# The causal mask in a decoder layer's self scores: sixteen bf16 products on 32 rows in place of four on 128

## The chip, the cores and the metric

The kernel runs on one core of a Trainium2 chip. The metric is the time of one execution on the device in microseconds (us). The profiled execution gives a span, from its first to its last instruction; the time of a run is longer by what lies around the span.

## The reference

One decoder layer over 32 batch rows of 128 tokens and 512 features: self attention with 16 heads of 32 features, rotary positions and a causal mask; cross attention to a context with fake int8 quantisation; a mixture of 64 experts with the best 8 for each token. Each of the three adds its result to its input. The part that matters:

```python
q = _rope(proj(Wq, bq)); k = _rope(proj(Wk, bk)); v = proj(Wv, bv)
att = jnp.einsum('bhqd,bhkd->bhqk', q, k) / scale
causal = jnp.tril(jnp.ones((t, t), bool))
att = jnp.where(causal, att, -jnp.inf)
att = jax.nn.softmax(att, axis=-1)
```

## The kernel before

The kernel has three stages. A setup loads the weights, splits most of them into a high and a low part, and loads small constants. The attention stage does one batch row (128 tokens on 128 partitions) a turn, 32 in all, with the work of several rows interleaved: a turn `cur` does the projections of row cur-1, the self attention of cur-2, the cross attention of cur-3 and cur-4, and the routing of cur-4 and cur-5. The expert stage then walks the 64 experts. It reads rows that GpSimd has scattered to `routed` in HBM, and adds the results to the output by indirect DMAs.

Each engine runs an order written out by hand in its `body(cur)`: on TensorE `turn_keys`, `positions`, `weigh_cross_1`, `turn_queries`, `turn_x`, `weigh_cross_3`, `_0`, `_2`, `turn_cross_keys`, `self_scores`, `turn_cross_attention`, `cross_values_b`, `turn_quantised_x` and so on. An engine waits on a semaphore where a step needs another engine's work (`reached`). The turns 1 to 6 and the last five are written out, those between are a loop.

The helper `scores` (L511) makes the scores of four groups of four heads in four banks of PSUM, 512 columns each: head 4i+j lies in bank j, columns 128i to 128i+127. Features of group j lie on partitions 32j to 32j+31, so the score products (L520) work on strips of 32 rows, one for each j, with fp32 operands, and stand in the profile with two records each. For the self scores (banks 2, 6, 3, 7) the mask comes first: L515 multiplies the identity `idb`, moving and read four times over, with the weights `mask_add` (128x128, bf16, 0 or -1e30), and starts the accumulation of each bank; the sixteen score products add to it. The cross scores (`wide_b`) have no mask.

Other lines that the prediction speaks of: L484 transposes in fp32, L489 transposes in bf16, L502 the fp32 projections, L508 the bf16 ones, L527 transposes of the probabilities, L534 their products with the values, and L545 and L546 the counts of positions. On VectorE L1269 takes the maximum of a bank of scores, L1311 and L1314 make the sum x2 behind the cross attention's output (`cross_scores` of TensorE waits for it), and L1479 and L1483 quantise x for `turn_quantised_x`. On ScalarE L1036 copies the turned cross keys. On GpSimd L1798 casts three constants to bf16 in the setup; TensorE waits for all of them (`s_init`) before its second turn. L1725 is a cast of the context. SP issues the loads: the constants behind the first four weight matrices, and later the filling of `routed` (`empty_row`, four DMAs of 5120 KB).

Of the kernel before, what the change touches and what calls it, by code (L numbers as in the profile page):

```python
# [31 lines left out]
BF16 = mybir.dt.bfloat16  # L32
# [5 lines left out]
P = 128  # L38
B = 32
D = 512  # L40
KT = D // P
H = 16
DH = D // H
# [59 lines left out]
def layer(nc, x, ctxT_in, qT_w, kT_w, vT_w, oT_w, xkT_w, xvT_w, xq_w, xp_w, biases, vb, xkb, xvb, ob, xbq, xbp, routerT,  # L103
# [4 lines left out]
    def sb(name, shape, dt=F32):  # L108
        return st.enter_context(nc.sbuf_tensor(name, shape, dt))
# [4 lines left out]
    with st:  # L114
# [6 lines left out]

        idf = sb("idf", [P, P])
        idb = sb("idb", [P, P], BF16)
        mask_add = sb("mask_add", [P, P], BF16)
        before = sb("before", [P, P], BF16)
        ones_b = sb("ones_b", [P, P], BF16)
        ones_f = sb("ones_f", [P, P])
        cos_sb = sb("cos_sb", [P, DH])
        sin_sb = sb("sin_sb", [P, DH])
        slot_base = sb("slot_base", [P, E])  # L130
# [42 lines left out]
        with ExitStack() as attention_only:  # L173
            def early(name, shape, dt=F32):
                return attention_only.enter_context(nc.sbuf_tensor(name, shape, dt))

            for name in ("q", "k", "v", "xk", "o", "xv"):
                W[name] = tuple(early(f"w_{name}_{part}", [P, KT, D], F32R) for part in ("hi", "lo"))
            roped = early("roped", [P, 2 * D])
            qT = early("qT", [P, NG, P])  # L180
            v_sb = early("v_sb", [P, D])
            xk_sb = early("xk_sb", [P, D])
            ctx_sb = early("ctx_sb", [P, D])
            turned_bias = early("turned_bias", [P, 2 * D])
            xv_bias = early("xv_bias", [P, D])
            xq_wT = early("xq_wT", [P, KT, D], BF16)
            xq8 = early("xq8", [P, D], BF16)
            xq8T = early("xq8T", [P, KT, P], BF16)
            att_bias = early("att_bias", [P, D])
            xv_sb = early("xv_sb", [P, D])  # L190
            probsT = early("probsT", [P, NG, GH * P])
            xp_wT = early("xp_wT", [P, KT, D], BF16)
            xo_tmp = early("xo_tmp", [P, D])[:, :]
            xo8 = early("xo8", [P, D], BF16)
            xo8T = early("xo8T", [P, KT, P], BF16)
            wide_a = early("wide_a", [P, 4 * D])
            row = early("row", [P, ROW])
# [149 lines left out]
        def _(sp):  # L347
# [12 lines left out]
            def load_constants():  # L360
                for dst, src_c in ((cos_sb, cos_t), (sin_sb, sin_t), (slot_base, slot0)):
                    sp.dma_start(dst[:, :], src_c).then_inc(s_const, 16)
                for k, src_c in enumerate((causal, prior)):
                    sp.dma_start(x3T[:, k * P:(k + 1) * P], src_c).then_inc(s_const, 16)
                sp.dma_start(xq_bs[:, :], xbq.rearrange("(g p) -> p g", p=P),
                             allow_slow_non_contiguous=True).then_inc(s_const, 16)
                sp.dma_start(v_bias[:, :], vb.rearrange("(g p) -> p g", p=P),
                             allow_slow_non_contiguous=True).then_inc(s_const, 16)
                sp.dma_start(xk_bias[:, :], xkb.rearrange("(g p) -> p g", p=P),
                             allow_slow_non_contiguous=True).then_inc(s_const, 16)  # L370
                sp.dma_start(xv_bias[:, :], xvb.unsqueeze(0).to_broadcast([P, D])).then_inc(s_const, 16)
                sp.dma_start(xatt[:, :], ob.unsqueeze(0).to_broadcast([P, D])).then_inc(s_const, 16)
                sp.dma_start(xp_bias[:, :], xbp.unsqueeze(0).to_broadcast([P, D])).then_inc(s_const, 16)
                sp.dma_start(router_w[:, :, :], routerT.rearrange("(t p) e -> p t e", p=P)).then_inc(s_const, 16)
# [105 lines left out]
        def _(pe):  # L480
# [30 lines left out]
            def scores(banks, q, keys, masked, done):  # L511

                if masked:
                    for b in banks:
                        pe.matmul(bank[:, b, :], idb[:, :], mask_add[:, :].unsqueeze(1).to_broadcast([P, GH, P]),  # L515
                                  start=True, stop=False)
                for i in range(NG):
                    for j, b in enumerate(banks):
                        own = slice(j * DH, (j + 1) * DH)
# [333 lines left out]
            def turn_quantised_weights():  # L853
# [17 lines left out]
                pe.wait_ge(s_wprep, 3)  # L871
                pe.wait_ge(s_att, 1)
                for g in range(KT):
                    last = pe.matmul(bank[:, 7, g * P:(g + 1) * P], ones_f[:, :], xn2[:, g * P:(g + 1) * P],
                                     start=True, stop=True)
                last.then_inc(s_wT, 1)

# [837 lines left out]
        def _(pool):  # L1715
# [72 lines left out]
            pool.iota(empty_row[:, D:ROW:2], pattern=[[0, E]], base=TOKENS, channel_multiplier=1,  # L1788
                      allow_small_or_imprecise_dtypes=True).then_inc(s_init2, 1)
            pool.memset(ones_b[:, :], 1.0).then_inc(s_init, 1)  # L1790
            pool.memset(ones_f[:, :], 1.0).then_inc(s_init, 1)
            pool.memset(chosen_before[:, :], 0.0).then_inc(s_init, 1)

            body(1)
            pool.wait_ge(s_ident, 16)
            pool.wait_ge(s_const, 16 * N_CONST)
            for dst, src in ((idb[:, :], idf[:, :]), (mask_add[:, :], x3T[:, 0:P]), (before[:, :], x3T[:, P:2 * P])):
                pool.tensor_copy(dst, src).then_inc(s_init, 1)  # L1798

            body(2)  # L1800
# [36 lines left out]
def tables():  # L1837
# [6 lines left out]
        "cos_t": np.concatenate([cos, cos], 1).astype(np.float32),  # L1844
        "sin_t": np.concatenate([-sin, sin], 1).astype(np.float32),
        "ident_f": np.eye(P, dtype=np.float32),
        "causal": np.where(p[None, :] > p[:, None], MASKED, 0.0).astype(np.float32),
        "prior": (p[:, None] < p[None, :]).astype(np.float32),
        "slot0": np.tile(np.float32(NOWHERE) - CAP * np.arange(E, dtype=np.float32), (P, 1)).astype(np.float32),
    }  # L1850
# [29 lines left out]
```

## Time and profile before

| | |
|---|---|
| time, median of 3 runs | 1783.19 us (1775.75 to 1784.44) |
| span of the profiled execution | 1569.0 us |
| TensorE (PE) busy | 1406.8 us, 90% |
| its weight loads (PEld) | 1063.2 us, 68% |
| VectorE (DVE) busy | 1168.0 us, 74% |
| ScalarE (ACT) busy | 971.5 us, 62% |
| GpSimd (POOL) busy | 673.1 us, 43% |
| mean granted clock of TensorE | 0.960 of full speed |
| mask products L515 | 128 records, 33.7 us busy |
| chain that ended last | PE 65%, DMA 23%, issue 5%, DVE 4% |

The shares are means over the three stages: setup and filling to about 100 us, attention to about 1100 us, experts to the end. Matmuls are pipelined: a record's duration includes the way through the array, so what one costs is read from the distance between starts, or from the chain, not from its duration.

### The profile page before, as it was taken

The page shows a single profiled execution, that of the slowest core. Times are in us where ns is not written, and L with a number is a line of the kernel's source. Part 1 is how long each engine was busy: PE and PEld are TensorE (multiplying, and loading weights), DVE is VectorE, ACT ScalarE, POOL GpSimd, SP SyncE. Part 2 cuts the span into 40 slices and gives each one's busy share as a digit, 9 for nine tenths or more (in the row PEclk, how much of TensorE's full clock was granted, in tenths as well). Part 3 has the DMA queues.
Part 4 walks back from the last instruction along what each step waited for, and adds up shares of the span by engine and source line. Part 5 has one row for each costly group of instructions (what it writes and reads, how often), then busy time and mean ns, then how long its engine had stood idle before and what let it go on. Part 6 is the DMA issues. An engine that isn't in the chain of part 4 may idle for free.

```text
span 1569.0 us, 35603 instructions
## 1 busy us (share of the span) xinstructions
PE 1406.8 (90%) x10963; PEld 1063.2 (68%) x10996; DVE 1168.0 (74%) x3111; ACT 971.5 (62%) x3345; POOL 673.1 (43%) x654
## 2 busy tenths in 40 slices
PE   3699999999999999999999999998619887888895
PEld 2467777777777777777777777776516565655573
DVE  5678889998999989999899999889524444444453
ACT  3357777777777777777777777777504333333342
POOL 0012444444444344453444534544343544555566
PEclk9799999999999999999999999999759999999997
DMA  9861332322111100111010111000597999999964
GB/s 283 347 237 35 131 125 101 105 98 107 66 46 45 34 27 27 34 34 40 27 27 27 34 43 30 27 21 21 191 331 214 292 249 287 281 276 281 261 99 51
DMA packets 159738, 195.81 MB, mean 125 GB/s; under 512 B 39541, under 2 KB 121845, under 8 KB 159680
## 3 DMA queue, kind: packets, MB, share of 16 engines
q1 hardware_dynamic: 120768, 157.27, 30.9%
q0 software_dynamic: 38912, 37.87, 11.8%
q8 instruction: 24, 0.39, 0.1%
q14 instruction: 34, 0.28, 0.1%
HBM read 127.60 MB, written 130.29 MB: 164 GB/s over the span
## 4 chain that ended last, share of the span: by engine, by line
PE 65%; DMA 23%; issue 5%; DVE 4%; ACT 1%; POOL 1%; SPq 1%; POOLq 0%; DVEq 0%
PE bank L502 33%; DMA out<-x,slots 20%; PE bank L527 7%; PE bank L484 7%; PE bank L520 5%; PE bank L534 4%; PE bank L508 3%; PE bank L540 2%; PE bank L515 2%; DMA x_in<-in_x 1%; PE bank L489 1%; DMA wide_b<-in_xkT_w 1%; POOL routed L1753 1%; DMA probsT<-in_oT_w 1%; ACT probs L966 1%
## 5 line engine op out<-in xcount | busy, mean ns | idle before, releaser
L966 ACT ACTIVATE probs<-bank,small 128x128 f32<-128x128 f32 x1024 | 362.1, 377 | 51.0 <-DVE small L1269 47.8
L1753 POOL DMA_INDIRECT routed<-row,slots x248 | 252.7, 1019 | 133.8 <-issue 74.0
L1822 POOL DMA_INDIRECT out<-x,slots x128 | 199.3, 1557 | 197.6 <-DMA out<-x,slots 137.4
L1718 POOL TENSOR_TENSOR small<-small,half 128x1 f32<-128x1 f32 x96 | 54.4, 567 | 523.3 <-DVE small L1241 523.3
L966 ACT ACTIVATION_READ_ACCUMULATOR probs<-bank,small 128x1 f32 x1024 | 220.7, 216 | 0.0
L960 ACT ACTIVATE probsT<-bank 128x512 f32<-128x512 f32 x256 | 144.1, 611 | 89.1 <-PE bank L527 89.1
L1269 DVE TENSOR_REDUCE small<-bank 128x4 f32<-128x512 f32 x256 | 166.7, 682 | 35.4 <-PE bank L520 35.4
L527 PE MATMUL bank<-idf,probs 128*128 128x128 f32 x1024 | 147.2, 277 | 2.4 <-ACT probs L966 2.4
L1673 DVE TENSOR_SCALAR slots<-pairs 128x1 uint32<-128x1 f32 x128 | 13.7, 149 | 174.7 <-DMA out<-x,slots 171.1
L527 PEld LDWEIGHTS bank<-idf,probs 128*128 128x128 f32 x1024 | 122.2, 144 | 26.8 <-DVE probs L1278 3.5
L1199 ACT ACTIVATE xn<-bank 128x192 f32<-128x192 f32 x64 | 21.3, 332 | 146.4 <-PE bank L906 146.4
L906 PE MATMUL bank<-w_gate_up,x_in 128*128 128x384 f32 x256 | 94.2, 514 | 0.3 <-issue 0.3
L1278 DVE TENSOR_TENSOR probs<-probs,small 128x512 f32<-128x512 f32 x128 | 89.9, 702 | 4.4
L906 PE MATMUL bank<-w_gate_up,x_res 128*128 128x384 f32 x256 | 92.6, 507 | 0.0
L906 PEld LDWEIGHTS bank<-w_gate_up,x_in 128*128 128x128 f32 x256 | 49.0, 202 | 29.7 <-issue 6.4
L906 PEld LDWEIGHTS bank<-w_gate_up,x_res 128*128 128x128 f32 x256 | 48.6, 200 | 27.9 <-issue 4.5
L502 PE MATMUL bank<-w_q_hi,xT_hi 128*128 128x512 f32 x128 | 57.7, 451 | 0.7 <-ACT xT_hi L960 0.7
L502 PE MATMUL bank<-w_o_hi,attT_hi 128*128 128x512 f32 x132 | 52.7, 399 | 3.5 <-DVE attT_lo L1626 2.4
L1679 DVE TENSOR_SCALAR x<-bank,pairs 128x256 f32<-128x256 f32 x128 | 55.4, 475 | 0.0
L502 PE MATMUL bank<-w_xv_hi,cT_hi 128*128 128x512 f32 x128 | 53.9, 421 | 0.4 <-ACT wide_b L1036 0.4
L502 PE MATMUL bank<-w_v_hi,xT_hi 128*128 128x512 f32 x128 | 54.0, 422 | 0.0
L502 PE MATMUL bank<-w_xk_hi,cT_hi 128*128 128x512 f32 x128 | 53.4, 417 | 0.0
(242 smaller groups left out, 3843.4 us busy)
## 6 DMA issues: line engine op xcount, KB each, us to landing
w_gate_up<-in_w_gate SPq DMA_DIRECT2D x128, 192.0 KB, 3.8
w_gate_up<-in_w_up SPq DMA_DIRECT2D x128, 192.0 KB, 4.0
w_down<-in_w_down SPq DMA_DIRECT2D x128, 192.0 KB, 4.4
routed<-empty_row SPq DMA_DIRECT2D x4, 5120.0 KB, 22.8
x_in<-in_x SPq DMA_DIRECT2D x32, 256.0 KB, 2.6
ctx_sb<-in_ctxT_in SPq DMA_DIRECT2D x32, 256.0 KB, 3.0
x_res<-in_x SPq DMA_DIRECT2D x32, 256.0 KB, 2.6
out<-x SPq DMA_DIRECT2D x32, 256.0 KB, 2.0
```

Of the source, the lines that this page charges most:

```text
L484: last = pe.transpose(bank[:, b, t * P:(t + 1) * P], src[:, t * P:(t + 1) * P], idf[:, :])
L502: done = pe.matmul(bank[:, b, :], lhsT, rhs, start=first and k == 0, stop=last and k == len(steps) - 1)
L520: last = pe.matmul(bank[:, b, i * P:(i + 1) * P], q[own, i, :], keys[own, i, :], start=not masked, stop=not masked or i == NG - 1)
L527: last = pe.transpose(bank[:, b, j * P:(j + 1) * P], probs[:, g, j * P:(j + 1) * P], idf[:, :])
L534: last = pe.matmul(bank[i * DH:(i + 1) * DH, b, g * P:(g + 1) * P], values[:, h * DH:(h + 1) * DH], probsT[:, g, i * P:(i + 1) * P], start ...
L906: last = pe.matmul(bank[:, 2 + k % 2, 0:2 * F], rowsT[k % 2][:, t * P:(t + 1) * P], w_gu[k][:, :, t, :], start=(t == 0), stop=(t == KT - 1))
L960: act.activation(dst, src, ACT.Copy).then_inc(done, 1)
L966: last = act.activation(probs[:, g, j * P:(j + 1) * P], bank[:, b, j * P:(j + 1) * P], ACT.Exp, bias=negated[:, h:h + 1], **({"accum_out": ...
L1269: dve.tensor_reduce(negated[:, g * GH:(g + 1) * GH], bank[:, b, :].rearrange("p (j k) -> p j k", j=GH), AX_X, ALU.max, negate=True).then_i ...
L1278: dve.tensor_tensor(heads, heads, own.unsqueeze(2).to_broadcast([P, GH, P]), ALU.mult).then_inc(d_norm, 1)
L1753: pool.indirect_dma_start(routed, bass.IndirectOffsetOnAxis(ap=slots_of(m)[:, k:k + 1], axis=0), row_of(m)[:, :], None, bounds_check=SLOTS ...
L1822: pool.indirect_dma_start(out.rearrange("b p (h c) -> (b p h) c", h=2), bass.IndirectOffsetOnAxis(ap=place_of[k % 2][:, half_:half_ + 1], ...
```

## The change

The mask becomes `mask_rows`, four tables of 128x128 side by side in bf16 (128 x 512): row p of table u holds the mask of key 32u + (p mod 32) for all 128 queries, so each strip of 32 partitions holds the same 32 keys. For each block u of 32 keys and each bank j, one product on the 32 rows of strip j adds the mask of these keys to the four heads of the bank: 32 x 128 weights, and a 32x32 piece of the identity read four times over as 128 moving columns, into four pieces of 32 columns of the bank. Sixteen products, u outside and j inside, in place of four. The constant grows from 128x128 to 128x512 fp32 and is loaded over the whole of `x3T`; the table `prior` goes to `v_sb` instead; and the fp32 ones, used once in the setup, move into `xk_sb`.

```diff
-        mask_add = sb("mask_add", [P, P], BF16)
+        mask_rows = sb("mask_rows", [P, NG, P], BF16)
...
-        ones_f = sb("ones_f", [P, P])
...
+            ones_f = xk_sb[:, 0:P]
...
-                for k, src_c in enumerate((causal, prior)):
-                    sp.dma_start(x3T[:, k * P:(k + 1) * P], src_c).then_inc(s_const, 16)
+                for dst, src_c in ((x3T[:, :], causal), (v_sb[:, 0:P], prior)):
+                    sp.dma_start(dst, src_c).then_inc(s_const, 16)
...
                 if masked:
-                    for b in banks:
-                        pe.matmul(bank[:, b, :], idb[:, :], mask_add[:, :].unsqueeze(1).to_broadcast([P, GH, P]),
-                                  start=True, stop=False)
+                    for u in range(NG):
+                        for j, b in enumerate(banks):
+                            own = slice(j * DH, (j + 1) * DH)
+                            pe.matmul(bank[:, b, :].rearrange("p (h k) -> p h k", h=GH)[:, :, u * DH:(u + 1) * DH],
+                                      mask_rows[own, u, :], idb[own, own].unsqueeze(1).to_broadcast([DH, GH, DH]),
+                                      start=(u == 0), stop=False)
...
-            for dst, src in ((idb[:, :], idf[:, :]), (mask_add[:, :], x3T[:, 0:P]), (before[:, :], x3T[:, P:2 * P])):
+            for dst, src in ((idb[:, :], idf[:, :]), (flat(mask_rows), x3T[:, :]), (before[:, :], v_sb[:, 0:P])):
                 pool.tensor_copy(dst, src).then_inc(s_init, 1)
...
-        "causal": np.where(p[None, :] > p[:, None], MASKED, 0.0).astype(np.float32),
+        "causal": np.stack([np.where((u * DH + p % DH)[:, None] > p[None, :], MASKED, 0.0) for u in range(NG)],
+                           1).reshape(P, D).astype(np.float32),
```

## Rows read from the trace of the kernel before

**Rows 1.** Windows: each engine's busy us and instructions, clock, DMA share.

```profile
core 0: us, PE busy (x) PEld busy (x) DVE busy (x) ACT busy (x) POOL busy (x), PEclk, DMA share, GB/s
62.00:92.00 30.00, 26.61 (x205) 19.29 (x203) 16.61 (x35) 13.36 (x48) 4.13 (x5) 0.95 1.03 385
...
200.00:400.00 200.00, 199.69 (x1753) 155.29 (x1757) 180.62 (x472) 155.94 (x577) 88.42 (x96) 1.00 0.29 103
...
617.50:650.30 32.80, 32.75 (x290) 25.45 (x290) 29.57 (x79) 25.45 (x95) 14.49 (x17) 1.00 0.11 32
```

**Rows 2.** The chain within one turn: start us, us, what and how many.

```profile
614.35 0.44 PE bank L484 x4
...
614.82 0.03 PE bank L546
...
617.60 0.86 PE bank L515 x4
618.47 1.10 PE bank L520 x32
...
621.08 0.24 PE bank L489 x4
```

**Rows 3.** The mask line's products from 62 to 92 us: ns, first and last start.

```profile
L515 PE MATMUL bank<-mask_add,idb x8: 379/498/634, 62.8 to 87.8; 128*128 128x512 bf16 x8
```

**Rows 4.** Timeline of TensorE and its loads at one mask: start us, us, group.

```profile
617.44 1.03 PE L515 MATMUL bank<-mask_add,idb 128*128 128x512 bf16 x4
...
618.39 0.98 PEld L520 LDWEIGHTS bank<-wide_a,qT 32*128 32x128 f32 x32 [0.42 <-issue]
...
618.09 0.38 PE L515 MATMUL bank<-mask_add,idb 128*128 128x512 bf16 x1
618.39 0.39 PE L520 MATMUL bank<-wide_a,qT 32*128 32x128 f32 x4
...
618.61 0.40 PE L520 MATMUL bank<-wide_a,qT 32*128 32x128 f32 x8
```

**Rows 5.** Timeline of TensorE behind the scores.

```profile
619.91 0.48 PE L502 MATMUL bank<-w_xv_hi,cT_hi 128*128 128x512 f32 x1
...
620.92 0.40 PE L489 MATMUL bank<-idb,xq 128*128 128x128 bf16 x4
```

**Rows 6.** Timelines of VectorE, ScalarE and the loads; in brackets the idle time before.

```profile
618.35 0.43 DVE L1483 TENSOR_SCALAR xq<-wide_b 128x512 bf16<-128x512 f32 x1
619.63 0.69 DVE L1269 TENSOR_REDUCE small<-bank 128x4 f32<-128x512 f32 x1 [0.85 <-PE bank L520]
...
617.64 1.14 ACT L1036 ACTIVATE wide_b<-bank,xk_bias 128x128 f32<-128x128 f32 x4
...
630.00 0.75 DVE L1311 SCALAR_TENSOR_TENSOR x<-bank,small,xp_row 128x512 f32<-128x512 f32 x1 [0.48 <-PE bank L508]
630.79 0.69 DVE L1314 TENSOR_TENSOR x<-x,wide_a 128x512 f32<-128x512 f32 x1
...
631.60 0.23 PEld L520 LDWEIGHTS bank<-wide_b 32*128 32x128 f32 x4 [0.40 <-issue]
...
1080.15 0.69 DVE L1269 TENSOR_REDUCE small<-bank 128x4 f32<-128x512 f32 x1 [0.43 <-PE bank L520]
```

**Rows 7.** The setup: the chain's long loads, a GpSimd cast of each size, TensorE's wait.

```profile
23.61 10.12 DMA probsT<-in_oT_w
...
74.39 15.65 DMA x_in<-in_x
...
23.41 0.29 POOL L1798 CAST mask_add<-x3T 128x128 bf16<-128x128 f32 x1
...
24.19 0.66 PE L484 MATMUL bank<-idf,xn 128*128 128x128 f32 x2 [24.19 <-POOL before L1798]
...
63.02 0.60 POOL L1725 CAST cT_hi<-ctx_sb 128x512 fp32r<-128x512 f32 x1
```

**Rows 8.** The chain behind the scores of the last turn.

```profile
1080.17 0.67 DVE small L1269
```

More of the change, by code:

```diff
@@ L873, in turn_quantised_weights @@
                 for g in range(KT):
-                    last = pe.matmul(bank[:, 7, g * P:(g + 1) * P], ones_f[:, :], xn2[:, g * P:(g + 1) * P],
+                    last = pe.matmul(bank[:, 7, g * P:(g + 1) * P], ones_f, xn2[:, g * P:(g + 1) * P],
                                      start=True, stop=True)
@@ L1790, in _ @@
             pool.memset(ones_b[:, :], 1.0).then_inc(s_init, 1)
-            pool.memset(ones_f[:, :], 1.0).then_inc(s_init, 1)
+            pool.memset(ones_f, 1.0).then_inc(s_init, 1)
             pool.memset(chosen_before[:, :], 0.0).then_inc(s_init, 1)
```

## The prediction

> **What bounds the kernel now.** I read the windows by stage first [rows 1]. In the attention stage, about 100 to 1078 us, TensorE is busy 199.69 of 200 us at a granted clock of 1.00; the DMA share is 0.29, later 0.11. One turn of the loop, that is one batch row, takes 32.80 us: TensorE is busy for 32.75 of it, VectorE for 29.6, ScalarE for 25.45, GpSimd for 14.5. So TensorE's own order of work sets the turn, and VectorE has some 3 us to spare. After 1078 us comes a tail, and then the experts, in which this code has no part.
>
> The chain of waits, read across one turn [rows 2], shows the same: one TensorE piece follows the other with nothing between. The four mask products (L515) are 0.86 us of it, and the 32 records of the score products (L520; two for each of the 16 fp32 products) are 1.10. The mask line holds 128 records, 4 in each of 32 turns; 8 of them, two turns, lie between 62 and 92 us [rows 3], the other 30 turns behind 100.
>
> **What the mask costs today.** The timeline of TensorE shows more than the 0.86 [rows 4]. The first mask product starts at 617.44, the last at 618.09; with 0.86 / 4 = 0.215 us each, its columns are in at 618.30. The first four score products are recorded at 618.39, the next four at 618.61, and from there to the end at 619.57 a group of four takes 0.11. The first group took 0.22 because its weight load, 0.11, could not be hidden: the load engine itself was idle for 0.42 before it [rows 4] and began only after 0.09 us of emptying, at the change from products on 128 rows to products on strips of 32. Thus the scores proper start at 618.61 - 0.11 = 618.50, and mask plus change of form take 618.50 - 617.44 = 1.06 us a turn.
>
> **What it will cost.** The sixteen products have 4 x 32 = 128 columns each, and go by fours: strips 0, 32, 64, 96 of rows, into banks 2, 6, 3, 7. The order is u outside, strip inside, the same as that of the score products. Those show that four products on four strips run beside each other: the four of the first group start within 0.02 us (they all stand in one piece at 618.39 [rows 4]), and 32 records of 128 fp32 columns take 1.10 us, where four records of 128 fp32 columns on all rows take 0.44 [rows 2]. So I count four rounds. A round of 128 bf16 columns I take from the bf16 transposes of L489, four in 0.24 us, 0.06 each [rows 2, 5]. The terms, from 617.44 on: emptying, now ahead of the mask, 0.09; the first bf16 weight load, not hidden, 0.05 (estimate: half of the 0.11 of fp32, bounded by 0.03, what a bf16 product with its own load takes in L546 [rows 2], and 0.11); four rounds 0.24; and the first fp32 load of the scores, 0.11, hides behind one round of 0.06 only, so 0.05. That makes 0.43. The scores follow in the same form of strips, without a second emptying. The gain is 1.06 - 0.43 = 0.63 us a turn. It comes from the columns (0.86 becomes 0.24); the loads that show stay about what they were (0.11 becomes 0.05 + 0.05), and so does the emptying.
>
> Bounds of this gain. Above: were the sixteen products free, 1.06 - 0.19 = 0.87. Below: were they to run one at a time at 0.06, 0.96 + 0.19 = 1.15, a loss of 0.09; at 0.11 each, a loss of 0.89. I stand near the upper part since the nearest row, the same four strips in the same order in the next line of code, overlaps.
>
> **Does the turn get 0.63 shorter?** The steps behind the mask wait for other engines, and these must keep up. VectorE reaches the first maximum of the scores (L1269) 0.85 us early and waits for L520 [rows 6]; this is the wait that shrinks, to 0.22, and it is the cover of the whole gain. Its next wait is 0.48 us ahead of L1311, for the cross output. L1314 then frees the cross scores on TensorE, which are loaded from 631.60 on, 0.12 us after L1314 ends at 631.48: a close finish, but both sides of it start from the same products (L508, whose end L1311 waits for), so both move alike [rows 6]. TensorE's next steps behind the scores take ScalarE's copies (L1036, ended by 618.79, and wanted by the products at 619.91) and VectorE's xq (done at 618.78, and wanted at 620.92) [rows 5, 6]: more than 1 us of room in each, of which 0.63 is used. Nothing else is late; GpSimd and the queues of SP are not moved, and no wait is added. With a gain of up to 0.85 the turn follows fully.
>
> Of the 32 turns, the first two lie in a stretch that ends with a load of x (15.65 us, 74.39 to 90.04) behind the filling of the routed rows, with a DMA share of 1.03 [rows 7]. What they gain there is waited away, so I count them at nothing; their cover is bandwidth, and without it they would add 2 x 0.63. In the last turn the chain leaves TensorE right after the scores and goes on in VectorE, which waited only 0.43 for them [rows 6, 8]: it gives 0.43. From there to the end the stages follow one another as before and start earlier by the sum. Total: 29 x 0.63 + 0.43 = 18.7 us.
>
> **Setup.** The mask constant grows from 64 to 256 KB, in as many DMA issues as before. 192 KB at the 385 GB/s that the stretch from 62 to 92 us moves [rows 1] is 0.5 us, and as the whole start hangs on DMAs, I count it in full. On GpSimd the cast of it grows from 128 to 512 columns: 0.29 us becomes about 0.60, the time of the 128x512 cast of L1725; TensorE's first product waits 24.19 us for these casts [rows 7]. That 0.3 is hidden, for the chain there runs over the weights (a load that lands at 33.74), not over TensorE; if it were not, it would be 0.3 more. That load, and with it the count of 0.5, is bounded by 0 and 0.8. The ones move into xk_sb, with the same memset, and are read at 52 us, ahead of the first keys; the second table goes to v_sb: nothing.
>
> **Sum.** The profiled execution spans 1569.0 us; the median of the runs is 1783.19, so 214.2 us lie outside the span, and the three runs lie between 1775.75 and 1784.44. 1569.0 - 18.7 + 0.5 = 1550.8, and with 214.2 it is 1765.0 us, 1.0% faster.
>
> **Rivals.**
> 1. A floor on the round. The fp32 group of four takes 0.11 [rows 4], and that may be the weight load as much as the columns; a load on 32 rows might take as long in bf16. Or each product costs a fixed start: L546, of 64 columns, takes 0.03 [rows 2], and 16 x 0.03 = 0.48. Either way the mask takes 0.65 to 0.67, the gain is about 0.40, and the time is 1783.2 - 30 x 0.40 + 0.5 = 1771.7. For it: no row has bf16 on strips. Against it: the starts inside a group lie within 0.02 us of each other. The Trainium skill (TensorE: Matmul & The Clock Gate, section "Wait — 56ns, not 53.3ns?") says that starts of matmuls never come closer than about 25 ns. By that, an estimate, the sixteen would take 0.40 us and the run would last about 1769.6; the group of four that starts within 0.02 us in this trace speaks against it for strips.
> 2. The change doesn't do what it says: bf16 products on strips with a target in pieces of 32 columns follow one another at 0.06. A turn loses 0.09: 1783.2 + 30 x 0.09 + 0.5 = 1786.4, no measurable change.
> 3. Slower: they follow one another, and each also waits for its own load, 0.11 a product, 16 x 0.11 + 0.19 = 1.95 us a turn, 0.89 lost: 1783.2 + 30 x 0.89 + 0.5 = 1810.4. It decides from the point at which a product costs more than (1.06 - 0.19) / 16 = 0.054 us. Against both 2 and 3 stands L520 [rows 2].
>
> **How the numbers follow.** Forecast 0.62, rival 1 0.22, rival 2 0.09, rival 3 0.07. The forecast's own spread: the gain of a turn from 0.50 to 0.85 (1769 to 1759), setup 0 to 0.8, some 3 us for the stretches at the lower clock, which can fall otherwise when the stages shift (the mean over the whole span is 0.960, over 62 to 92 us 0.95 [rows 1]). 1756 to 1778 takes in the forecast and rival 1 with their spread. A measurement tells about 0.5% (9 us) from no change; below 1774.3 is faster. The forecast and nearly all of rival 1 lie there: 0.81 faster; same 0.12 (rival 2 and the rest of rival 1); slower 0.07 (rival 3).
>
> **What the profile will show.** Right: the mask line with 512 records on 32 rows, some 0.3 us in the chain per turn where it was 0.86; idle of the load engine ahead of it instead of ahead of L520; VectorE's wait at L1269 near 0.2 us; a turn of 32.2 us with TensorE still busy throughout; the experts' stage as long as before. Wrong: a turn of 32.4 means rival 1; a turn not shorter, with products 0.06 apart, rival 2. If the mask is short but the turn stays above 32.2, the gain went into a wait for VectorE, and my reading of its 0.85 us was wrong.

## The result: 0.8% slower, and what the profile after shows

In runs side by side the kernel before takes 1782.49 us (median of 8, 1775.61 to 1787.34) and the changed kernel 1795.51 us (median of 8, 1792.22 to 1805.46): ratio 1.0084 with an interval of 1.0057 to 1.0111. The prediction was 1765.0 us, faster. It was wrong in sign.

The page of the changed kernel, its span, busy times and the chain that ended last:

```profile
span 1791.5 us, 36404 instructions
PE 1481.8 (83%) x11380; PEld 1110.6 (62%) x11380; DVE 1166.3 (65%) x3111; ACT 975.0 (54%) x3345; POOL 672.8 (38%) x654
...
DVE 27%; PE 22%; DMA 19%; another core or an unknown queue 14%; issue 13%; ACT 2%; SPq 1%; DVEq 1%; POOL 0%; POOLq 0%
```

The chain was 65% TensorE before and is 22% now. A window of the changed kernel (columns as in [rows 1]):

```profile
200.00:400.00 200.00, 172.37 (x1410) 132.04 (x1411) 145.27 (x376) 124.65 (x462) 69.82 (x76) 0.93 0.24 88
```

And two successive mask pieces in its timeline of TensorE (start us, us, group):

```profile
607.91 0.40 PE L517 MATMUL bank<-idb,mask_rows 32*128 32x128 bf16 x16
...
648.91 0.40 PE L517 MATMUL bank<-idb,mask_rows 32*128 32x128 bf16 x16
```

TensorE is busy 172.37 of 200 us where it was 199.69 [rows 1], and a turn, from one mask to the next, takes 41.00 us (the median of the turns with a scatter is 41.02) where it was 32.93. (The 32.80 of [rows 1] is the width of that window.) That is +8.1 us in nearly every turn, some 220 us in all, from a change that was to move a turn by less than 1 us.

The span itself solves half of this. 1791.5 us belongs to an execution of 1793.32: only 1.8 us lie around a span. In every other run below it is 1.8 or 1.9 us. So the 214.2 us that the prediction had "outside the span" are not there. The profile of before (span 1569.0) and the timed runs of before (1783.19) are executions at two levels of speed, and it was the other level that was timed. Across the experiments the kernel before took 1567.6 and 1568.5 us on two chips (called free below), and 1784.7 to 1788.5 on two others, and 1782.5 in the measurement above (called stalling). No chip showed both. On which chip the measurement above ran isn't on record; it can be one of the two stalling ones, or a third. On a stalling chip, the kernel before unchanged (e6_before) spans 1786.6 us, and its window and its timeline of TensorE look like this:

```profile
200.00:400.00 200.00, 173.30 (x1382) 131.96 (x1389) 146.94 (x385) 126.11 (x464) 69.43 (x76) 0.91 0.23 86
```

```profile
606.38 1.03 PE L515 MATMUL bank<-mask_add,idb 128*128 128x512 bf16 x4
607.34 1.17 PE L520 MATMUL bank<-wide_a,qT 32*128 32x128 f32 x32
608.45 0.76 PE L484 MATMUL bank<-idf,xatt 128*128 128x128 f32 x4
...
617.88 0.80 PE L502 MATMUL bank<-w_q_hi,xT_hi 128*128 128x512 f32 x1 [5.45 <-DVE xatt L1285]
...
647.00 1.03 PE L515 MATMUL bank<-mask_add,idb 128*128 128x512 bf16 x4
```

Nothing of this is in [rows 1 to 8]: the turn is 41 us already before the change, and TensorE stands still for 5.45 us behind the scores, waiting for VectorE's xatt.

Why VectorE is late there: its own timeline in that turn, then GpSimd's (e6_before; in brackets the idle time before and what ended it).

```profile
613.27 0.69 DVE L1269 TENSOR_REDUCE small<-bank 128x4 f32<-128x512 f32 x1 [5.55 <-remote]
616.85 0.25 DVE L1283 RECIPROCAL small<-small 128x16 f32<-128x16 f32 x1 [2.89 <-remote]
```

```profile
605.94 1.10 POOL L1753 DMA_INDIRECT routed<-row,slots  x1 [1.38 <-DVE chosen_before L1351]
607.34 1.23 POOL L1753 DMA_INDIRECT routed<-row,slots  x1 [0.30 <-issue]
...
615.26 0.97 POOL L1753 DMA_INDIRECT routed<-row,slots  x1 [0.30 <-issue]
```

The score products have all started and stand as done by 608.51 (607.34 + 1.17). VectorE, which waits for the first bank of them, starts at 613.27, 4.8 us later, and the releaser is given as "remote": no instruction in the trace ends just before. In [rows 6] the same instruction had an idle time of 0.85 us, and L520 ended it. In the events of the trace, TensorE's first signal of the scores comes 3.3 us after its product has ended here (611.82; VectorE starts 0.02 us behind the second, 613.25), and the steps behind it signal up to 7.6 us late; outside this stretch the distance is 0.014 us. The stretch goes with one thing: GpSimd issues the scatter of the routed rows, eight indirect DMAs (L1753) from 605.94 to 616.2. As long as they are issued, and up to 1.5 us behind, semaphore signals of TensorE arrive late, those of the scores about 1.4 us apart. Of the other engines' signals most are recorded on time in the same stretch (VectorE's at 613.98 and ScalarE's at 615.51, each 0.01 us behind its step). Some have no event at their end at all; whether those came late the trace doesn't tell.

The changed kernel in its turn, TensorE's timeline first, then VectorE's:

```profile
607.91 0.40 PE L517 MATMUL bank<-idb,mask_rows 32*128 32x128 bf16 x16
608.15 1.05 PE L523 MATMUL bank<-wide_a,qT 32*128 32x128 f32 x22
609.46 0.47 PE L523 MATMUL bank<-wide_a,qT 32*128 32x128 f32 x3 [0.27 <-issue]
610.20 0.49 PE L523 MATMUL bank<-wide_a,qT 32*128 32x128 f32 x4 [0.28 <-issue]
610.91 0.49 PE L523 MATMUL bank<-wide_a,qT 32*128 32x128 f32 x3 [0.22 <-issue]
...
619.98 0.79 PE L502 MATMUL bank<-w_q_hi,xT_hi 128*128 128x512 f32 x1 [4.74 <-DVE xatt L1288]
```

```profile
614.68 0.69 DVE L1272 TENSOR_REDUCE small<-bank 128x4 f32<-128x512 f32 x1 [5.51 <-remote]
618.94 0.25 DVE L1286 RECIPROCAL small<-small 128x16 f32<-128x16 f32 x1 [3.57 <-remote]
```

The mask is as short as forecast: the scores start 0.24 us after it (608.15 - 607.91), where it was 0.96 (607.34 - 606.38 above). But now the score products themselves break up. They come in groups 0.7 us apart with "issue" ahead of them, the last group starts 3.00 us behind the first mask product (610.91 - 607.91), where in e6_before even the step behind the scores starts at 2.07 (608.45 - 606.38); and the maximum of the scores, counted from the first mask product, starts 6.77 us later (614.68 - 607.91) where it was 6.89 in e6_before. Of the 0.7 us that the mask gives, 0.1 is left in this turn. The waits of VectorE for late signals from 200 to 1200 us (us in total, times, longest), first for the scores and then for the step behind them, in the changed kernel:

```profile
DVE small L1272 <- remote: 163.2, 24, 9.6
...
DVE small L1286 <- remote: 54.3, 23, 3.6
```

and in e6_before:

```profile
DVE small L1269 <- remote: 134.0, 24, 6.9
...
DVE small L1283 <- remote: 72.2, 23, 3.6
```

The two go together: 217.5 us in the changed kernel, 206.2 in e6_before. The later the first signal, the less is left to wait for the second. (The two traces may be of two chips; pairs on one chip follow.)

### The profile page after: what moved, and what is told of

Its sections match the earlier page's. It is cut to its first block, busy times and chain, and to the rows that moved or that the text cites. A ratio compares the mean times of both kernels' runs of the same rounds, so it can differ in the third digit from the quotient of the medians.

```text
span 1791.5 us, 36404 instructions
## 1 busy us (share of the span) xinstructions
PE 1481.8 (83%) x11380; PEld 1110.6 (62%) x11380; DVE 1166.3 (65%) x3111; ACT 975.0 (54%) x3345; POOL 672.8 (38%) x654
## 3 DMA queue, kind: packets, MB, share of 16 engines
q0 software_dynamic: 38912, 37.87, 10.3%
## 4 chain that ended last, share of the span: by engine, by line
DVE 27%; PE 22%; DMA 19%; another core or an unknown queue 14%; issue 13%; ACT 2%; SPq 1%; DVEq 1%; POOL 0%; POOLq 0%
DMA out<-x,slots 16%; PE bank L502 12%; PE bank L508 3%; DVE small L1239 3%; DVE small L1272 2%; DVE xn L1258 2%; DVE wide_a L1308 2%; PE bank L530 2%; PE bank L484 2%; DVE x L1314 1%; DVE small L1262 1%; DVE xatt L1288 1%; PE bank L909 1%; DVE x L1439 1%
## 5 line engine op out<-in xcount | busy, mean ns | idle before, releaser
L502 PE MATMUL bank<-w_q_hi,xT_hi 128*128 128x512 f32 x128 | 74.0, 578 | 123.7 <-DVE xatt L1288 120.2
L502 PEld LDWEIGHTS bank<-w_q_hi,xT_hi 128*128 128x128 f32 x128 | 31.1, 243 | 144.2 <-DVE xatt L1288 126.6
L909 PE MATMUL bank<-w_gate_up,x_in 128*128 128x384 f32 x256 | 92.7, 507 | 0.3 <-issue 0.3
L523 PE MATMUL bank<-wide_a,qT 32*128 32x128 f32 x1024 | 70.9, 296 | 20.3 <-issue 20.3
L523 PEld LDWEIGHTS bank<-wide_a,qT 32*128 32x128 f32 x1024 | 52.7, 190 | 32.5 <-issue 32.3
L502 PE MATMUL bank<-w_k_hi,xT_hi 128*128 128x512 f32 x128 | 66.2, 517 | 1.8 <-ACT xq8T L963 1.8
L502 PE MATMUL bank<-w_q_lo,xT_hi 128*128 128x512 f32 x128 | 63.6, 497 | 0.0
## 6 DMA issues: line engine op xcount, KB each, us to landing
routed<-empty_row SPq DMA_DIRECT2D x4, 5120.0 KB, 23.2
```

The lines of the kernel that those rows point to most:

```text
L502: done = pe.matmul(bank[:, b, :], lhsT, rhs, start=first and k == 0, stop=last and k == len(steps) - 1)
L523: last = pe.matmul(bank[:, b, i * P:(i + 1) * P], q[own, i, :], keys[own, i, :], start=not masked, stop=not masked or i == NG - 1)
L909: last = pe.matmul(bank[:, 2 + k % 2, 0:2 * F], rowsT[k % 2][:, t * P:(t + 1) * P], w_gu[k][:, :, t, :], start=(t == 0), stop=(t == KT - 1))
```

## The experiments

All times are medians against the kernel before on the same chip, with the ratio and its interval. A turn is the median distance from one mask to the next in the turns with a scatter. Line numbers of a variant are shifted by up to some ten lines.

### Is the 214 us part of the change? e1_before, e5_after, e6_before, e10_after

No edit: the two kernels as they are.

> The kernel before, unchanged. The changed kernel's span was 1791.5 us in a run of 1793.3, so only 1.8 us lie around a span, while the profile of before shows 1569.0 against a median of 1783. Theory S (stall): most executions of before have the same stall that the changed kernel's trace shows (in 27 of 32 turns TensorE's signals behind the self scores come 5 to 9 us late, a turn lasts 41 instead of 33 us), and the profiled one of 1569 was a rare one without it; then this profile spans about 1780, with turns near 40 us. Theory P (profile as it stands): before has no stall, turns last 32.9 us, and 212 us lie around the span; then the span is again 1569.

1569.55 us beside 1567.64 (ratio 1.0008, 0.9990 to 1.0026), turn 32.93: a free chip, no stall. The span agrees with theory P, but the time with neither, since nothing lies around the span.

> The kernel before, for a trace of it on this chip. Theory C: at about 1783 us its trace shows the stall behind the self scores, turns of some 40 us; at 1568 us none, turns of 32.93 us. Theory S1: no stall in it, turns of 32.9 us, on either level.

1790.68 us, span 1786.6, turn 41.04: a stalling chip. The 217.6 us between the spans 1786.6 and 1569.0 lie in the turns from the fourth mask on: 28 of them, 40.78 us in the mean where they took 32.91, 220 us in all. The first scatter starts with the fourth mask (156.0 and 156.3 us); the three turns ahead of it take their old time.

> The changed kernel, unchanged, beside before on one chip. The kernel before took 1783 us beside the changed one and 1568 us in the first four experiments: the level differs from chip to chip. Theory C (the chip decides whether the stall is there): where before takes about 1568, the changed kernel has no stall either, turns of 32.3 us, about 1549 us; where before takes about 1783, it takes about 1795 again. Theory S1 (scatter and dense burst collide, on any chip): the changed kernel stalls here too and takes about 1795 us, whatever before takes.

1818.32 us beside 1788.54 (1.0162, 1.0133 to 1.0190), turn 41.69, on the same chip as e6_before: 27.6 us slower than that. 24.7 us lie between the first mask and the last (1260.06 us, 62.18 to 1322.24, against 1235.35, 62.80 to 1298.15); the rest lies behind the attention. VectorE's two waits are 218.3 + 4.6 = 222.9 us here and 134.0 + 72.2 = 206.2 in e6_before.

> The changed kernel, unchanged. Chip without the stall (before about 1568 us): theory C (the chip decides) says turns of 32.30 us and about 1549 us, faster by 1.2%; theory S1 in its strong form (the denser burst brings the stall even where before has none) says turns of 41 us and about 1795 us. Chip with the stall: 1795 to 1820 us, as before.

1799.60 us (1.0110, 1.0061 to 1.0158) on a second stalling chip, turn 40.97. What the change costs on a stalling chip lies between 0.8 and 1.6%; its sign was the same in all three measurements.

### What is the mask's work worth? e4_no_mask

```diff
-                    scores((2, 6, 3, 7), qT, kT, True, p_s)
+                    scores((2, 6, 3, 7), qT, kT, False, p_s)
```

The mask is left out of the computation.

> The kernel before without the mask products: the scores start their banks themselves, and the attention is not causal (this part of the computation is left out). Theory S2: the burst shrinks to 16 products like that of the cross scores, which shows no stall; turns of 31.9 us, about 1540 us. Theory S1: the scores still lie beside the scatter, so the stall remains; a turn is at most 0.9 us shorter, 1750 to 1783 us. Theory P: 1783 - 31 x 0.96 = 1753 us.

1544.41 us beside 1567.64 on a free chip (0.985, 0.9829 to 0.9870), 23.2 us. The whole mask is worth that much there, and a gain of 18 to 19 us was all but the most that could be had.

### Does the scatter do it? e12_after_no_scatter, e13_before_no_scatter

In both kernels the eight indirect DMAs of a turn, and the waits on them, are taken away. The scatter of the rows is thus left out of the computation.

```diff
-                for k in range(TOPK):
-                    pool.indirect_dma_start(routed, bass.IndirectOffsetOnAxis(ap=slots_of(m)[:, k:k + 1], axis=0), row_of(m)[:, :], None,
...
```

> The kernel before without the scatter (left out: the experts get no rows). If the scatter is the cause: turns of 32.93 us on every chip, and the changed kernel without it is faster by 18 to 20 us, the gain of the working of the prediction (18.2).

> The changed kernel without the scatter of the routed rows (left out: the experts get no rows). On every chip, if the scatter is the cause: turns of 32.30 us, no late signal. If something else delays the signals: turns of 41 us remain on a chip with the stall. The attention stage is what counts; the expert stage may take another time, as its rows are all empty.

On a stalling chip, on which the kernel before takes 1787.47 us, e13 takes 1564.94 (0.8751) and e12 1545.86 (0.8644). All of the stall is gone, as the expectations said, and with it the sign of the change: it is 19.1 us faster, turns of 32.93 become 32.27. Windows of e13 and e12, in this order:

```profile
200.00:400.00 200.00, 199.69 (x1760) 155.32 (x1767) 179.66 (x472) 155.85 (x570) 39.29 (x48) 1.00 0.10 32
```

```profile
200.00:400.00 200.00, 199.69 (x1891) 156.97 (x1896) 183.78 (x483) 157.91 (x582) 42.41 (x52) 1.00 0.11 33
```

TensorE is full in both, as in [rows 1]. The wait that the prediction named as the cover, VectorE's for the scores (from 200 to 1000 us: us in total, times, longest), in e13 and in e12:

```profile
DVE small L1265 <- PE bank L518: 22.8, 24, 0.9
```

```profile
DVE small L1268 <- PE bank L521: 7.0, 25, 0.3
```

0.95 us a turn becomes 0.28, so 0.67 us of cover were used, and cover was left.

### Does less of it do less? e14_after_half_scatter

The changed kernel scatters for 4 of the 8 chosen experts.

```diff
-                for k in range(TOPK):
+                for k in range(4):
```

> The changed kernel with four of the eight indirect DMAs of each scatter (left out: half of the routed rows). Chip with the stall: the signals come back when the issue ends, some 5.1 us earlier than with eight, so the stall of 8.5 to 9.3 us a turn shrinks to 3.5 to 4.5, turns of 36 to 37 us, about 1655 us. Theory T (the stall has a fixed length once it is set off): turns of 41 us. Chip without: turns of 32.3 us.

1648.93 us (0.9231, 0.9193 to 0.9269), turn 36.00: 3.7 us over the 32.27 of no scatter, where eight cost 9.4 on this chip (e5_after, 41.69). VectorE's wait for late signals is still there:

```profile
DVE small L1272 <- remote: 92.7, 22, 4.2
```

4.2 us a turn (92.7 / 22), where it is 9.5 (218.3 / 23) with all eight (e5_after, the same chip). The delay grows with the number of indirect DMAs, and the time is the one expected; a stall of fixed length would have left the turn at 41 us.

### Does the place matter? e2, e3 (free chip), e8, e9 (stalling chip)

Steps that compute nothing of use hold GpSimd for 4.14 us ahead of the scatter, so that it falls behind the scores. In e8 and e9 the last turns are left as they are, since the experts wait for them. The edit of e2 and e3; in e8 and e9 a condition on the turn stands behind `range(6`:

```diff
                 reached(pool, d_r2, m, 6, 6)
+                for k in range(6):
+                    until(pool, s_idle, nth(m, 6, k))
+                    pool.tensor_tensor(idle_out[:, :], half[:, :], half[:, :], ALU.pow).then_inc(s_idle, 1)
```

> The changed kernel, with six small power operations (0.57 us each, some 3.9 us with their waits) on GpSimd ahead of each row's scatter, so that its eight indirect DMAs start some 3.4 us behind the first mask product instead of 0.5 us ahead of it. Theory S1 (the scatter's issue and the dense burst of small products collide): no stall, turns of 32.2 us, about 1550 us. Theory S2 (the burst of 16 + 16 products alone outruns TensorE's instruction supply, whatever GpSimd does): turns stay at 41 us, about 1795 us. Theory S3 (the scatter stalls TensorE wherever it lies): the stall moves with it, 1780 to 1800 us.

> The kernel before, with the same 3.9 us of GpSimd work ahead of each scatter. Theory S1: no stall, turns of 32.9 us, about 1572 us. S2: before's burst has 4 + 16 products, the stall stays as it is in before, about 1783 us. S3: 1780 to 1800 us. Theory P: about 1783 us, as the scatter is no bound.

On a free chip e2 takes 1562.95 us, e3 1582.52: the change gives 19.6 us there, in turns of 32.30 beside 32.99. (e3 is 14.9 us longer than the kernel before with turns only 0.05 longer. In its trace the last scatter ends at 1180.5 us, 13.4 later than in e1_before, where the last mask comes 4.7 later: most of the time goes at the end, where the experts wait for the scatter.) As there is no stall on this chip either way, the two say nothing about its cause.

> The kernel before with the same delay in the same turns. Chip without the stall: turns of 32.98 us, 1567 to 1571 us, some 19 us above the changed kernel with the delay, which is then the pure price of the four mask products against the sixteen. Chip with the stall: S1 says none, about 1570 us; S3 says 1750 to 1800 us.

> The changed kernel with 3.9 us of GpSimd work ahead of the scatter, but only in the turns that have a mask (rows up to 29), so that the tail isn't delayed. On a chip where before takes about 1568 us: turns of 32.30 us and 1546 to 1552 us. On a chip where before takes 1783 to 1790 us: theory S1 (the late signals need a scatter that is under way while the burst of masks and self scores runs) says no stall, turns of 32.3 us, about 1550 us, 13% faster than before; theory S3 (while the scatter runs, TensorE's signals are late whatever it does) says that the signals behind the cross values and projections come late in place of those of the scores, turns of 38 to 41 us, 1750 to 1800 us.

On a stalling chip (before 1784.72) e9, the kernel before with a late scatter, takes 1652.39 us (0.9308, 0.9237 to 0.9378), turn 35.27, and e8, the changed one, 1724.74 (0.9697, 0.9644 to 0.9749), turn 38.41. Both beat both kernels, and neither lies in a range that was expected (about 1550 to 1570 us, or 1750 to 1800); e9 is the fastest with the whole work done on such a chip. The waits of e9 and of e8 (us in total, times, longest):

```profile
ACT xo8T L962 <- remote: 27.1, 21, 2.2
```

```profile
ACT wide_b L1071 <- remote: 78.1, 24, 4.3
...
ACT xo8T L965 <- remote: 50.5, 25, 3.6
```

The scores' signals are on time in both, the delay has moved on with the scatter and meets other waits. They are longer in e8, 3.3 and 2.0 us a time against 1.3, though its mask products are over before the scatter starts; why, these runs don't tell. So the cure works in both, and in part only: without any scatter the two kernels take 1545.86 and 1564.94 on the other stalling chip.

### Is it the number of products, their form or their order? e11_before_split16, e7_after_by_bank

e11 keeps the mask of before, 128 rows and the 128x128 table, and cuts each product of 512 columns in four of 128: sixteen products, the same columns.

```diff
-                    for b in banks:
-                        pe.matmul(bank[:, b, :], idb[:, :], mask_add[:, :].unsqueeze(1).to_broadcast([P, GH, P]),
-                                  start=True, stop=False)
+                    for h in range(GH):
+                        for b in banks:
+                            pe.matmul(bank[:, b, h * P:(h + 1) * P], idb[:, :], mask_add[:, :],
+                                      start=(h == 0), stop=False)
```

> The kernel before with each of its four 512-column mask products cut into four of 128 columns on the same 128 rows: as many instructions as the changed kernel, as many columns as before. Chip without the stall: the same time as before within 0.3%, turns of 32.9 to 33.0 us. Chip with it (before 1783 to 1790 us): theory B (a backlog that grows with the number of TensorE's instructions while the scatter is issued) says as slow as the changed kernel, 1800 to 1815 us; the rival F (the lost time hangs on when TensorE gets there, or on the form on strips) says as before, 1783 to 1792 us.

1813.66 us beside 1787.47 (1.0139, 1.0097 to 1.0182), turn 41.65. This is the loss of the changed kernel on that chip (1818.32, turn 41.69) without strips and without a changed table. Its wait:

```profile
DVE small L1270 <- remote: 210.2, 23, 9.9
```

9.1 us a turn (210.2 / 23), beside 9.5 in e5_after and 5.6 (134.0 / 24) in e6_before, all on one chip. With the second wait, for the step behind, it is 219.0 us in all, beside 222.9 and 206.2; it is this sum that moves with the time. Twelve more products in this place, each with its own weight load, make the loss, and not their form.

In e7 the two loops of the changed mask are swapped, bank by bank instead of strip by strip.

```diff
-                    for u in range(NG):
-                        for j, b in enumerate(banks):
+                    for j, b in enumerate(banks):
+                        for u in range(NG):
```

> The changed kernel with the sixteen mask products bank by bank instead of block by block, so that four in a row lie on one strip and do not overlap. The working of the prediction: each costs 0.056 us alone, 0.9 us in all, so a turn is 0.67 us longer than that of the changed kernel, 32.9 to 33.0 us and about 1568 us if nothing stalls. Theory S2 (a burst denser than the instruction supply stalls TensorE): where the changed kernel stalls, this one, with 16 products over 0.9 us instead of 0.23, stalls less or not at all. Theory S1: it stalls as the changed kernel does, since its scores lie beside the scatter as before.

1813.05 us (1.0144, 1.0111 to 1.0178), turn 41.64: as e5_after. In a turn without a scatter, at 122 us, the mask piece is the same length too:

```profile
123.25 0.43 PE L517 MATMUL bank<-idb,mask_rows 32*128 32x128 bf16 x16
123.48 1.15 PE L523 MATMUL bank<-wide_a,qT 32*128 32x128 f32 x32
```

The scores start 0.23 us behind the first mask product here, 0.24 with strips in turn. The expectation that the order would cost 0.9 us was wrong: the turn is 32.24 us and was 32.20. On the disputed point, whether products of 128 bf16 columns on 32 rows run beside each other, this says that the sixteen cost a quarter of their columns in either order (0.23 us, where sixteen at the 0.06 of the prediction would be 0.96). The products of one strip in a row start 12 to 15 ns apart there, once 26.

### Is it GpSimd's rate of issue? e15, e16, e17, e18 (a free chip)

One idle step and a wait stand ahead of each of the eight indirect DMAs, in the changed kernel (e15) and in that of before (e16).

```diff
                 for k in range(TOPK):
+                    until(pool, s_idle, nth(m, 8, k))
+                    pool.tensor_tensor(idle_out[:, :], half[:, :], half[:, :], ALU.pow).then_inc(s_idle, 1)
+                    until(pool, s_idle, nth(m, 8, k + 1))
+                    apart(pool)
                     pool.indirect_dma_start(routed, bass.IndirectOffsetOnAxis(ap=slots_of(m)[:, k:k + 1], axis=0), row_of(m)[:, :], None,
...
```

> The changed kernel with one small GpSimd operation (0.6 us with its waits) ahead of each of the eight indirect DMAs, so the issue takes some 15 us in place of 10. Theory B (a backlog of TensorE's records and signals is served only between the issues): the signals drain in the gaps, the stall shrinks below that with the late scatter, turns of 34 to 37 us, 1600 to 1680 us. If the delay only follows the time until the last indirect DMA: turns of 44 to 47 us, above 1880 us. Chip without the stall: about 1550 to 1565 us.

> The kernel before with the same spacing. Theory B: fewer instructions than in the changed kernel, so not slower than it on a chip with the stall: 1590 to 1670 us. Chip without: 1570 to 1585 us.

The chip turned out a free one (before 1568.49), and yet they take 1801.13 and 1796.45 us (1.1480 and 1.1458), turns of 39.70 and 39.63. Waits of e15, of the lines with a part in it:

```profile
POOL routed L1762 <- POOL idle_out L1759: 116.5, 136, 0.9
ACT row L984 <- DVE small L1412: 106.0, 18, 8.2
...
PE bank L486 <- DVE attT_lo L1271: 94.5, 18, 7.6
DVE small L1251 <- POOL small L1723: 74.7, 17, 6.8
```

No "remote" among them: this is another loss. GpSimd spends 2.5 to 2.8 us on each DMA instead of 1.3, comes 6.8 us late with a small step of the next row's norm (L1723), and VectorE, ScalarE and TensorE wait in a row. So the pair doesn't test theory B, and that e15 would take at most 1565 us without a stall, and e16 at most 1585, was a miss: I had counted the idle steps as free because GpSimd has the time in the sum ([rows 1], 14.5 of 32.8 us), though not in that place.

The late scatter with ten steps (e17) and with three (e18), on the kernel before:

> The kernel before with ten small GpSimd operations (6.5 us) ahead of the scatter in the turns with a mask, in place of six, which gave 1652 us. The issue then lies some 5.7 to 16 us behind the first mask product, and takes in the burst of the cross scores at 14 us. Theory B: that burst is delayed as the self scores' was, and the time is above 1652 us, 1680 to 1750. If only the self scores' place matters: 1640 to 1655 us.

> The same with three operations (2 us), so that the issue starts 1.2 to 1.5 us behind the first mask product, within the scores. Theory B: between before and six operations, 1680 to 1780 us. If it matters only that the first indirect DMA comes behind the burst's start: about 1652 us.

1698.15 us (1.0829, 1.0797 to 1.0862), turn 37.44, and 1571.64 us (1.0015, 0.9999 to 1.0030), turn 32.99. Three steps cost nothing on a free chip, ten too much. In e17 too GpSimd's small step of the next row's norm comes right behind the last indirect DMA, and TensorE waits for VectorE (37.1 us in 20 turns, 200 to 1000 us, for `roped`); the steps between were not followed. That 1698 lies within the range of theory B says nothing for it: that range was for a chip with the stall, and no wait of e17 is "remote". How either does on a stalling chip was not run, so six steps are not known to be the best.

## Why the prediction was wrong, point by point

**The step that failed is in the sum: "so 214.2 us lie outside the span".** The prediction took a difference of 12% between the profiled execution and the timed runs for something that lies around the span, which nothing in the trace shows, and carried it along as a constant. It was the price of a stall in 28 turns, in the part of the kernel that the change touches: 1.8 us lie outside the span. Against a span + 1.8 us, [rows 1 to 8] are those of a free chip, and their sum reads 1569.0 + 1.8 - 18.7 + 0.5 = 1552.6. That is the forecast which they carry; it says nothing of 1783.

**"TensorE's own order of work sets the turn" [rows 1]: right on a free chip, wrong where it was timed.** There the turn ends through the late signals: scatter, signal of the scores, VectorE's maximum and xatt, then TensorE's L502, which waits 4.7 to 5.5 us. The 3 us to spare of VectorE are gone. The prediction had the stall at nothing, both what it costs (8.1 us a turn) and what twelve more products add to it (0.6 us a turn net, e5 and e6).

**"Nothing else is late; GpSimd and the queues of SP are not moved, and no wait is added": the words are true of the program, and were no ground.** GpSimd's scatter starts 0.4 to 0.5 us ahead of the mask (605.94 and 606.38; 607.39 and 607.91), and more TensorE instructions in its reach cost more. The scatter had no row in the argument at all.

**The gain of 0.63 us a turn: right, and 0.04 to 0.06 too small.** The chain of the changed kernel in a turn without a scatter, beside [rows 2]:

```profile
122.33 0.59 PE bank L484 x4
122.91 0.33 PE bank L517 x16
123.25 0.95 PE bank L523 x32
```

Mask and scores take 1.28 us where they took 0.86 + 1.10 = 1.96: 0.68. As turns it is 32.933 - 32.266 = 0.667 (e13, e12) and 32.987 - 32.300 = 0.687 (e3, e2). The total, forecast 18.7 less 0.5 for the setup, is 19.1 and 19.6. The turn itself is 32.27 us where 32.2 was announced, because the prediction started from 32.80, the width of its window, and not from 32.93. The load engine's timeline:

```profile
122.84 0.23 PEld L517 LDWEIGHTS bank<-idb,mask_rows 32*128 32x128 bf16 x16 [0.17 <-issue]
123.03 0.98 PEld L523 LDWEIGHTS bank<-wide_a,qT 32*128 32x128 f32 x32
```

The emptying and the first load now stand ahead of L517, as said; the idle time is 0.17 where it was 0.42 [rows 4]. All sixteen loads pass in 0.23 us, so four rounds of 0.06. Rival 1, a floor on the round or on each product, fell with it: sixteen products would have taken 0.48. So did rivals 2 and 3.

**The cover of 0.85 us [rows 6]: right.** 0.67 of it were used (e12, e13); L1310's wait for L506, which stands for L1311, stayed at 11.9 us in 25 turns, 0.48.

**Setup and the first turns: small, as said.** The first mask product comes at 63.55 where it was 62.81, with 62.18 (e5_after) to 64.13 (e17_before) in other kernels of either form; 0.5 us can't be told in this.

**The rivals and the range.** None of the three had the cause: all were prices of the sixteen products themselves. 1795.51 lies beyond the upper end of 1778, and between rivals 2 and 3 by number only. "Slower" had a chance of 0.07, for another reason. A rival that would have met it was at hand, "the timed runs are not at the level of the profile, so the bound is unknown", and its range would have been wide.

**What is still open.** The runs show that late signals go with the scatter's issue (e12 to e14), follow its place (e8, e9) and grow with the number of TensorE instructions there (e11, on one chip). They don't show by what the two meet. It wasn't tried to give TensorE's scores fewer signals. Why two chips do without the stall is open. The scatter itself is as fast on both kinds: one indirect DMA each 1.28 us, and the packets of its kind of queue take 11.8% of 1569.0 us and 10.3% of 1791.5, 185 us both times. But the traces themselves differ: on the free chips, and in the profile of before, at most 5 of a trace's semaphore events are missing, counted against the instructions that raise them; on the stalling chips 129 to 434 are, and 136 and 129 even in e12 and e13, which have no scatter and no stall. So something in the recording differs between the chips, and whether it has a part in the stall, and whether an execution that nobody records has it at all, stays open: every time of the experiments comes with a span and a clock. The changed kernel as it is was never run on a free chip; that it would be faster there, by 1.2%, is argued from e2 against e3 and e12 against e13, not shown.

## What to carry to other kernels

Subtract the span from the time of its own execution before anything else; if the timed runs differ from both by more than a few us, the profile shows another level, and no sum made from it holds for them. A saving on an engine is worth its time only where the engine is the bound at the level that is timed. And where signals of an engine are held up as here, its count of instructions was the price (1.4% for twelve products more, e11), not its columns: join small products rather than split them, or move the issue of the indirect DMAs to a stretch where fewer wait (7% here, e9).

## What the runs showed of the hardware that I had not expected

- On two of the four chips that are on record, and in the first measurement, TensorE's semaphore signals come late while GpSimd issues indirect DMAs (one each 1.28 us): those of the scores up to 8.2 us, about 1.4 us apart. The matmul records of the kernel before show no gap in the same stretch. On the other two chips no signal is late.
- On the same chips semaphore events are missing from the traces (129 to 434 a trace, at most 5 on the others), also without the scatter.
- In the same stretch, with sixteen mask products where there were four, the score products behind them break up into groups about 0.7 us apart, with 0.22 to 0.28 us of "issue" ahead of each. It is so in e11 as well (14.7 us of such waits ahead of the scores, 55 times from 200 to 1200 us; once, 0.3 us, in e6_before).
- Sixteen bf16 products on strips of 32 rows and 128 columns take 0.23 us, in the records of the trace 2 to 5 ns between the starts of a group of four and 0.056 us from group to group (0.067 from the first to the second). By the Trainium skill (TensorE: Matmul & The Clock Gate, section "Wait — 56ns, not 53.3ns?") starts come no closer than about 25 ns; the rows of the changed kernel show them closer on strips.
- The idle time costs clock as well. TensorE's mean granted clock from 200 to 400 us is 0.93 in the changed kernel and 1.00 in [rows 1]; behind the wait of 4.74 us the products of L502 start 0.42 us apart (the second 0.59 behind the first), where those ahead of it stood 0.23 apart, and the window right behind it shows the lower of the two levels, 1.2 GHz (clock 0.50; columns as in [rows 1]):

```profile
620.00:622.00 2.00, 2.00 (x5) 1.61 (x6) 1.97 (x5) 0.85 (x5) 0.00 (x0) 0.50 0.00 0
```
